# Moving two projections, four output parts and the moves of the second head half within a pipelined attention batch

## The reference, cut to what matters

```python
q = (src @ Wq + bq).reshape(B, T, 16, 16)       # src is xn
k = (src @ Wk + bk).reshape(B, T, 16, 16)
v = (src @ Wv + bv).reshape(B, T, 16, 16)
scores = jnp.einsum('bqhd,bkhd->bhqk', q, k) * 16 ** (-0.5)
probs = jax.nn.softmax(scores, axis=-1)
attn = jnp.einsum('bhqk,bkhd->bqhd', probs, v).reshape(B, T, 256)
x = _layer_norm(src + attn @ Wo + bo, ln1_g, ln1_b)
keys = (x @ router_w + router_b)[..., 0]        # picks one of 4 experts for each row
...
result = x_in + rotary_attention(xn) + layer_norm(x + expert(x))
```

## Time and profile before

| what | value |
|---|---|
| median of 3 runs | 1951.32 us (1950.38 to 1961.06) |
| the profiled execution, its own time | 1956.04 us |
| its span in the trace | 1954.2 us |
| TensorE busy | 1776.0 us, 91% |
| DVE busy | 1302.0 us, 67% |
| POOL busy | 985.4 us, 50% |
| ACT busy | 828.7 us, 42% |

### The profile page before, as it was taken

One profiled execution on the slowest core, in us unless ns is written; L12 is line 12 of the kernel. 1 busy time (PEld: TensorE's weight loads), 2 busy tenths in 40 slices (PEclk: granted clock), 3 DMA queues, 4 the chain that ended last, 5 costly groups with the idle time before them and its releaser, 6 DMA issues.

```text
span 1954.2 us, 32195 instructions
## 1 busy us (share of the span) xinstructions
PE 1776.0 (91%) x11513; PEld 1057.9 (54%) x11514; DVE 1302.0 (67%) x2920; ACT 828.7 (42%) x1140; POOL 985.4 (50%) x645
## 2 busy tenths in 40 slices
PE   4989999999987399995799999999999999999998
PEld 2334334434443399995555646556565565654654
DVE  5767788778775477776765666656666577565760
ACT  2546556555543144443243341532524425244242
POOL 1133454355257144444467384573854738737464
PEclk7889999999988699997799999999999999999999
DMA  6547637646632655664000100101001010010100
GB/s 111 91 135 122 107 116 138 105 113 127 117 130 116 245 196 218 217 220 131 24 1 1 44 1 12 33 1 44 1 12 34 1 44 1 9 36 1 33 1 11
DMA packets 81440, 151.52 MB, mean 78 GB/s; under 512 B 11638, under 2 KB 55318, under 8 KB 75420
## 3 DMA queue, kind: packets, MB, share of 16 engines
q1 hardware_dynamic: 77980, 141.12, 27.9%
q0 software_dynamic: 3072, 8.39, 1.3%
q10 hardware_dynamic: 256, 0.26, 0.1%
HBM read 84.47 MB, written 39.85 MB: 64 GB/s over the span
## 4 chain that ended last, share of the span: by engine, by line
PE 42%; DVE 4%; POOL 3%; issue 2%; ACT 1%; DMA 0%; POOLq 0%; DVEq 0%; SPq 0%
PE a_psO L745 12%; PE a_psS L731 11%; PE a_psO L768 5%; PE a_psM L705 4%; PE a_psS L693 4%; PE a_psS L677 3%; PE a_psS L758 3%; DVE a_junk L551 2%; ACT a_probs L479 1%; POOL a_q_tok L366 1%; POOL a_k_tok L366 1%; DVE a_probs L521 1%; DVE a_probs L527 1%; POOL a_oT L389 0%; POOL a_probs L401 0%
## 5 line engine op out<-in xcount | busy, mean ns | idle before, releaser
L401 POOL TENSOR_TENSOR a_probs<-a_probs 128x1024 f32<-128x1024 f32 x144 | 341.7, 2400 | 294.1 <-PE a_psO L745 294.1
L551 DVE CUSTOM_DVE_ANT_0 a_junk<-a_psM,a_alibi 128x512 bf16<-128x512 f32 x512 | 333.2, 689 | 193.5 <-PE a_psM L705 193.5
L1349 DVE TENSOR_REDUCE f_n_tok<-f_psR 128x1 f32<-128x512 f32 x512 | 325.8, 682 | 99.7 <-PE f_psR L1584 96.8
L479 ACT ACTIVATE a_probs<-a_psS 128x1024 f32<-128x1024 f32 x256 | 248.8, 1024 | 271.6 <-PE a_psS L731 270.8
L1293 ACT ACTIVATE f_probs<-f_psS 128x1024 f32<-128x1024 f32 x256 | 248.0, 1023 | 143.7 <-PE f_psS L1603 140.1
L745 PE MATMUL a_psO<-a_probs,a_v 128*32 128x512 f32 x2048 | 244.0, 597 | 0.0
L1584 PE MATMUL f_psR<-f_kP,f_qP 48*128 48x512 f32 x512 | 167.4, 523 | 54.2 <-DVE f_n_tok L1349 34.9
L1584 PEld LDWEIGHTS f_psR<-f_kP,f_qP 48*128 48x128 f32 x512 | 66.0, 196 | 231.1 <-issue 103.7
L1616 PE MATMUL f_psO<-f_probs,f_v 128*32 128x512 f32 x1024 | 144.0, 636 | 1.8 <-issue 1.7
L705 PE MATMUL a_psM<-a_kH,a_qH 64*128 64x512 f32 x512 | 123.1, 476 | 23.9 <-DVE a_n_tok L551 23.4
L768 PE MATMUL a_psO<-a_wo,a_oT 128*128 128x256 f32 x512 | 125.3, 390 | 4.4 <-POOL a_oT L389 4.4
(11 more groups left out here) (212 smaller groups left out, 3535.2 us busy)
## 6 DMA issues: line engine op xcount, KB each, us to landing
w_w_high<-w_parts SPq DMA_DIRECT2D x23, 1024.0 KB, 5.6
w_w_low<-w_parts SPq DMA_DIRECT2D x23, 1024.0 KB, 7.6
sorted_rows<-f_zeros SPq DMA_DIRECT2D x6, 1408.0 KB, 5.6
f_kP<-f_high SPq DMA_DIRECT2D x64, 128.0 KB, 5.9
f_qP<-f_high SPq DMA_DIRECT2D x64, 128.0 KB, 7.6
f_w_raw<-in_L_ffn_W SPq DMA_DIRECT2D x16, 512.0 KB, 5.3
w_parts<-f_w_high SPq DMA_DIRECT2D x16, 512.0 KB, 2.7
w_parts<-f_w_low SPq DMA_DIRECT2D x16, 512.0 KB, 4.3
```

Source lines behind the costliest of these rows:

```text
L401: nc.gpsimd.tensor_tensor(slots, slots, probs[:, first - GRP:first - GRP + 2, :], ALU.add).then_inc(added.sem, 1)
L479: nc.scalar.activation(probs[:, slots, :], psS[:, 2 * p:2 * p + 2, :], ACT.Exp).then_inc(exp_done.sem, 1)
L551: nc.vector.tensor_tensor_reduce(out=junk[:, a, :], in0=psM[:, a, :], in1=alibi[:, h, :], scale=1.0, scalar=-3.0e38, op0=ALU.add, op1=ALU.max,
L1349: nc.vector.tensor_reduce(n_tok[:, c, column:column + 1], psR[:, ring_bank("max", batch, u), :], AX.X, ALU.max, negate=True).then_inc(max_ ...
```

## The change

It does four things. (1) The projections of sides 2 and 3 go from periods 6 and 7 to periods 12 and 13; in period 13 side 3 stands ahead of the next batch's first maxima row. (2) The four output parts go from periods 8, 9, 11, 12 to 6, 7, 9, 10. (3) POOL's list is reordered to fit: after `normalize(b, 0)` come `add_bias_to_rows` and `keep_rows`, and `low_part` 2 and 3 come after `normalize(b, 1)`, ahead of the first `split_chunk`, of `scale_rows` and of all that follows. SP's `move_sides(b + 1, 1)` goes behind the first chunk's store and load and `load_rows`. (4) DVE's work between the units is shifted: the inverse sums of quad 0 to period 5 and of quad 1 to period 10, `norm1.aggregate` from period 12 to 10, `weigh_rows` from period 5 to 12. The last batch has a table of its own, which is not edited.

```diff
     EXTRAS = {(0, 1): [("v", 1), ("maxima", 1)], (1, 0): [("proj", 0)], (1, 1): [("proj", 1), ("maxima", 2)],
-              (1, 2): [("proj", 2)], (1, 3): [("proj", 3)], (2, 0): [("out", 0)], (2, 1): [("out", 1), ("maxima", 3)],
-              (2, 3): [("out", 2)], (3, 0): [("out", 3)], (3, 1): [("maxima", 0)], (3, 3): [("v", 0)]}
+              (1, 2): [("out", 0)], (1, 3): [("out", 1)], (2, 1): [("out", 2), ("maxima", 3)], (2, 2): [("out", 3)],
+              (3, 0): [("proj", 2)], (3, 1): [("proj", 3), ("maxima", 0)], (3, 3): [("v", 0)]}
...
                 clear_rows(b)
                 move_sides(b + 1, 0)
-                move_sides(b + 1, 1)
                 for i, n in enumerate(chunks_of(b)):
                     sp.wait_ge(n_moved.sem, n_moved.at(*((b + 1, 0) if i else (b, 3))))
                     if n:
                         store_chunk(n - 1)
                     load_chunk(n)
-                    if i == 0 and b + 2 < B:
-                        load_rows(b + 1)
+                    if i == 0:
+                        if b + 2 < B:
+                            load_rows(b + 1)
+                        move_sides(b + 1, 1)
...
                 normalize(b, 0)
                 if more:
-                    low_part(b + 1, 2)
-                    low_part(b + 1, 3)
+                    add_bias_to_rows(b, not before)
+                    keep_rows(b + 1)
                 else:
                     norm1.raise_aggregate(pool, b - 1)
                     scatter_rows(0, 3, 8)
                 normalize(b, 1)
                 if more:
-                    add_bias_to_rows(b, not before)
-                    keep_rows(b + 1)
+                    low_part(b + 1, 2)
+                    low_part(b + 1, 3)
                     for n in chunks_of(b)[:1]:
                         split_chunk(n)
                     if before:
...
-                elif at == (1, 1) and b >= 2:
+                elif at == (1, 1):
+                    turn_sums(b, 0)
+                elif at == (2, 2):
+                    invert_sums(b, 1)
+                elif at == (3, 0) and b >= 2:
                     weigh_rows(b - 2, (0, 1))
-                elif at == (1, 2):
-                    turn_sums(b, 0)
-                elif at == (2, 3):
-                    invert_sums(b, 1)
...
-                elif at == (1, 1) and b >= 2:
+                elif at == (1, 1):
+                    invert_sums(b, 0)
+                elif at == (3, 0) and b >= 2:
                     weigh_rows(b - 2, (2, 3))
-                elif at == (1, 2):
-                    invert_sums(b, 0)
...
-                    if more and before and at == (3, 0):
+                    if more and before and at == (2, 2):
                         norm1.aggregate(dve, b - 1)
```

## The result

The changed kernel takes 1967.88 us in the median of 9 runs (1965.95 to 1971.28), the kernel before 1952.5 us in 9 runs beside it. The ratio is 1.0076, with a 95% interval from 1.0064 to 1.0088: 15 us slower. The spans of the two profiled executions are 1966.1 and 1954.2 us, 11.9 apart; the profiled execution of before was itself 3.5 us above its median.

What follows compares the result with a forecast made beforehand. POOL's list, not TensorE, was taken to set each batch's turnover. Batch 1 +0.9, batches 2 to 6 +7.2 and clock +1.8 gave +9.9 us: 1961 from the 1951.3 median; own range 1954 to 1971, 8 in 10 from 1949 to 1975.

Steps and rivals of the forecast that it cites:

- the sum: Whole kernel: batch 1 +0.9, batches 2 to 6 +7.2, clock +1.8, batch 0 nothing; together +9.9 us.
- POOL's list behind low part 3 sets the turnover: End of each batch: low part 3 ends at 329.23, then 20.80 and 2.76 us to the next transposes; +1.43 us a batch.
- The periods' lengths: Periods 8 to 13 of a batch: 2.85, 4.68, 4.40, 2.85, 4.80 and 5.42 us, with bounds for 10 and 12.
- Batches 1 to 5: Turnovers: batch 1 +0.9 us, having no weigh_rows, later ones +1.43 each; clock 0.3 a batch on top.
- The clock: TensorE behind the period 3 wait: a longer wait adds 0 to 1.7 us of half clock; 0.3 a batch taken, 1.8 in all.
- Batch 0: Its turnover: maxima row stall goes, but chunk rounds queue behind moves running to about 119; 0 taken, bounds -5 and +3.
- signs that I had named for being wrong: Early low part 3; POOL waiting for a load before the second split; period 0 waiting for maxima; batch 0 moving several us.
- Batch 6 and the last: Last batch's first output part waits for POOL's normalize (1.53 us) behind batch 6's list, so batch 6's delay goes through.
- The stuck maxima row: Rival, 18%: period 13's maxima row is held up amid the moves and period 0 waits; 1.7 us a batch more, 1971.
- The faster rival: Rival, 8%: extras cost 4.24 us flat, low part 3 ends at 326.9, 0.9 before today's split; 1941.
- today's split: Start of POOL's first split in the kernel before, at 327.80; low part 3 was forecast to end 1.43 us behind it.
- The moves of the second half: Last six issued from 329.2, ending near 337, needed about 340.3 in period 1; hidden with 3 us to spare, cost 0.

Runs made afterwards that it cites:

- 0.9941: The changed kernel with projections 2 and 3 one period sooner, in periods 11 and 12; 1937.46 us, ratio 0.9941 to the kernel before.
- 0.9904: The kernel before with output parts 2 and 3 a period sooner, in periods 10 and 11; 1931.43 us, ratio 0.9904.
- 0.9924: The kernel before with output parts 2 and 3 a period sooner, and weigh_rows moved from period 5 to period 7; ratio 0.9924.

## Why the prediction was right, point by point

The forecast was the measured outcome, slower and inside the range; 1961 was said, 1967.88 measured. From profile to profile the sum said 9.9 us more and 11.9 came. The rest of the miss lies in the 4.7 us that I took off because the profiled execution of before ran above its median: the changed kernel's own ran at its median.

- **POOL's list behind low part 3 sets the turnover.** Right: moving low part 3 sooner, or shortening what stands behind it, made the kernel faster, and moving `weigh_rows` alone did not. In batch 3 low part 3 was to end 47.98 us behind the transposes (329.23 - 281.25) and ended at 47.98 (338.23 - 290.25); 71.54 us a batch was said and 71.50 measured. That it came out to the hundredth was luck: period 8 started 0.2 us sooner than assumed, the periods from 8 to 12 and low part 3 behind the start of 13 came 0.2 later, and in the batches from 1 to 6 the low part ended between 47.91 and 48.80.
- **The periods' lengths.** Said, then measured: period 8 2.85 and 2.85; period 9 4.68 and 5.02; 10 4.40 and 4.40; 11 2.85 and 2.94; 12 4.80 and 4.47; 13 5.42 and 5.49. The errors of 9 and 12 cancel. Period 9 starts behind an empty one, and its scores take 0.96 instead of 0.62 us; with an output part in period 8 it took 4.70. Period 12 was mis-costed: I put 0.56 us on it for `weigh_rows`, which cost it nothing (4.47 with and without). What is above 4.24 goes with the empty period 11: with an output part there, and no `weigh_rows`, it took 4.25.
- **Batches 1 to 5:** 6.6 us plus 1.5 for the clock were said, 8.6 measured. Take out what the half clock costs at the start of each batch, and the turnover grew by 1.35, 1.61, 1.61, 1.91 and 1.58 us, 8.1 in all, where 6.6 was said; the clock gave 0.55 instead of 1.5. The two errors cancel.
- **The clock:** sized at 1.8 us over six turnovers. Over 3.73 us from the transposes to the first projection, the six batches from 1 to 6 lose 6.6 us before and 8.7 in the changed kernel; counting the slow projection of 3.60 us in the earlier trace rows, before loses 8.3. The longer waits cost 0.4 us more, not 1.8. What I missed is the other direction: a wait that is gone altogether gives back the whole loss.
- **Batch 0:** 0 was said, +3.1 measured, at the upper bound. Mis-sized was the end of the moves' data: I had it at about 119, but SP was still issuing them until 119.7 and their data ran to about 123, so the load behind them was used 7.4 us after its issue instead of 5.3. Two of the signs that I had named for being wrong did show, both in batch 0 alone: POOL waited for a chunk's load ahead of the second split (8.19 us, before 1.59), and the turnover moved by 3 us.
- **Batch 6 and the last:** the two waits did grow, the one for the first output part from 1.53 to 2.28 us and the one in period 3 from 2.44 to 3.16, and behind the one in period 3 the last batch stood 1.4 us later, where the sum had 1.7. But the stretch came out 1.1 us shorter in this pair of profiles, mainly since the half-clock stretches fell otherwise: the last batch's output part 3 took 1.99 us, at a granted clock of 1.00, where it had taken 3.78 at 0.50. Whether it would in other executions is not shown.
- **The stuck maxima row** did not come: period 0's scores show no wait. ACT issued the row's DMAs from 337.24 to 338.49, and SP's next store, which waits for them among others, left at 343.20, while the moves' data ran on to between 347 and 348. So the row landed within 4.7 us of its last issue, and not behind the whole backlog. That it passed the moves issued ahead of it is not shown: those were six, at 1.0 us each from about 335.4, done near 341.5. The rule that the Trainium skill gives (DMA: Bandwidth & Descriptors, "Queues, rings and completion order") is neither shown nor refuted by this row, and the 7.3 us of batch 0 in the kernel before stay open.
- **The faster rival** needed low part 3 to end before today's split. It did not, by 1.4 us. Its own sum was wrong as well: projection 3 stands ahead of the maxima row in period 13, so the 1.18 us of that row do not delay low part 3, and with the other three savings it would have ended at 328.07, still 0.27 behind. The run with 0.9941 is what lies on the other side of that point.
- The moves of the second half hid, as said, in batches 1 to 5; the spare was nearer 2 us than the 3 that I gave. In batch 3 the rate of the moves, some 130 GB/s, ends between 347 and 348, and the max unit ran at 349.45.
- **The range:** its upper bounds add up to more than the +20 that I gave: 12.6 us for the periods of six batches and up to 10.2 for the clock are about +23. The measured time lies inside either.

The profiles account for 11.9 of the 15.4 us between the medians; the other 3.5 are the profiled execution of before, which ran that much above its median. Why it did is not known.

## What to carry to other kernels

When an engine's list in program order sets the turnover, as POOL's did here, cost a reordering by the last item that has to wait for someone and by the work that stands behind it, not by the work moved. Look for the one item whose move by a single period takes the wait away: here two output parts, one period sooner, were worth 1%, while the large reordering lost 0.8%. Before filling an engine's idle time, ask what the engine beside it is reading then.

## What the runs showed of the hardware

A DVE instruction with two SBUF inputs (the dot product of a row tile with the router's weights) was held up by the POOL instruction that ran beside it and ended about 0.3 us behind its end: 0.59 to 1.53 us instead of 0.41, and in the last batch of before one of 2.57 us beside a split of 2.42. A POOL instruction that started while a dot product ran took about 0.2 us longer (1.23 instead of 1.04). DVE's reductions out of PSUM were not lengthened (1.28 us), and neither were dot products beside POOL's indirect DMAs in the last batch (0.42). The Trainium skill (SBUF — State Buffer, "Who interferes with whom") says that a DVE instruction with two SBUF inputs contends with a GpSimd instruction that reads SBUF, and that reductions never contend; the traces agree on the first (1.25 us and more instead of 0.41), and on the second for reductions that read PSUM (1.28 us).

TensorE's granted clock fell to 0.50, the 1.2 GHz level, behind the waits of period 3 in most batches (from 292 to 294 in batch 3 of the changed kernel), and it stayed at 1.00 through batches 2 to 5 of the three versions without that wait (0.9941, 0.9904 and 0.9924). TensorE's idle time of 1.6 to 2.5 us there thus cost another 1.4 us a batch on average, in the kernel before as in the changed one.

Left open: why the second chunk's load holds POOL up longer in batches 1 and 2 (3.12 and 3.39 us) than in batches 3 to 5 (1.66, 1.64 and 1.96) of the version with the split ahead and `weigh_rows` in period 5. The chunks up to batch 3's first are parts of W2 and the later ones of W1, read by differently shaped DMAs, and the step falls at that place; but no run tested it.
